# One-hots in three batches of 42, 42 and 41 slots a chunk with two buffers, in place of five of 25 with three; the gates' weights loaded later

## The reference

```python
h = relu(layernorm(x))                                    # layer 0
norm = clip(out_degree(src), 1, None) ** -0.5
x = x + relu(segment_sum((h * norm)[src], dst)) @ W.T + b
h = relu(layernorm(x))                                    # layer 1
msg = h[src] @ W_msg.T + b_msg + edge_embed[edge_type]    # 9 types
m = segment_sum(msg, dst)
r = sigmoid(m @ Wih_r.T + h @ Whh_r.T + biases)           # GRU cell
z = sigmoid(m @ Wih_z.T + h @ Whh_z.T + biases)
n = tanh(m @ Wih_n.T + b + r * (h @ Whh_n.T + b))
x = x + (1 - z) * n + z * h
```

## Time and profile before

| | |
|---|---|
| Runs | 997.35 us median of 3 (994.53 to 997.53) |
| Profiled execution | 993.72 us, its span 991.9 us |
| PE busy | 852.4 us, 86% |
| PEld busy | 758.8 us, 77% |
| DVE busy | 808.3 us, 81% |
| ACT busy | 515.5 us, 52% |
| POOL busy | 74.4 us, 8% |
| PE matmul groups | L1063 437.2 us, L1074 422.1, L1196 277.0 |
| Mean granted TensorE clock | 0.975 |

### The profile page before, as it was taken

The page is one execution under the profiler, slowest core; times in us unless marked ns, Lnnn a source line. Parts: engine busy times, 40 slices in busy tenths (PEclk is TensorE's granted clock), DMA queues, the critical chain, the costliest instruction groups (busy, mean ns, idle before and its releaser), DMA issues.

```text
span 991.9 us, 21125 instructions
## 1 busy us (share of the span) xinstructions
PE 852.4 (86%) x8908; PEld 758.8 (77%) x8908; DVE 808.3 (81%) x1177; ACT 515.5 (52%) x1051; POOL 74.4 (8%) x71
## 2 busy tenths in 40 slices
PE   1333599898998998989989999989999999999993
PEld 1222488787887887878878888969888889888882
DVE  5959999999999999999999995267766667766666
ACT  2896278687886886868868887211111111111110
POOL 5860100100101001000000000000000000000000
PEclk9999889999999999999999999999999999999997
DMA  4623315443434544333534330266667776666740
GB/s 108 143 68 130 132 50 221 159 159 136 159 141 159 227 174 159 137 137 147 212 134 187 140 141 7 60 237 242 245 245 266 280 269 245 241 246 260 280 162 12
DMA packets 38739, 169.99 MB, mean 171 GB/s; under 512 B 8156, under 2 KB 21667, under 8 KB 35696
## 3 DMA queue, kind: packets, MB, share of 16 engines
q1 hardware_dynamic: 32486, 161.48, 43.2%
q0 software_dynamic: 6000, 6.48, 2.8%
q10 hardware_dynamic: 154, 0.64, 0.2%
HBM read 88.52 MB, written 80.00 MB: 170 GB/s over the span
## 4 chain that ended last, share of the span: by engine, by line
PE 55%; DVE 29%; ACT 11%; issue 3%; DMA 2%; SPq 0%; DVEq 0%
PE ps L1196 25%; PE ps L1074 13%; DVE work L691 9%; DVE work L698 7%; PE ps L1063 7%; ACT ring L881 5%; DVE work L704 2%; PE ps L1162 2%; PE ps L1163 2%; ACT junk L893 2%; DMA tab<-dst 1%; PE ps L1086 1%; PE ps L1167 1%; PE ps L1166 1%; PE ps L1100 1%
## 5 line engine op out<-in xcount | busy, mean ns | idle before, releaser
L1063 PE MATMUL ps<-work 128*128 128x106 f16 x3125 | 437.2, 217 | 86.4 <-ACT ring L881 66.9
L1074 PE MATMUL ps<-ring,tab 125*128 125x250 f16 x2500 | 422.1, 275 | 1.9 <-DVE tab L676 1.2
L881 ACT ACTIVATE ring<-ps 128x848 f16<-128x848 f32 x375 | 330.0, 882 | 98.1 <-PE ps L1063 92.2
L1063 PEld LDWEIGHTS ps<-work 128*128 128x128 f16 x3125 | 291.4, 102 | 108.0 <-ACT ring L881 67.2
L1196 PE MATMUL ps<-ring,tab 125*128 125x250 f16 (+1 forms) x2500 | 277.0, 269 | 0.0
L1074 PEld LDWEIGHTS ps<-ring,tab 125*128 125x128 f16 x2500 | 246.9, 99 | 28.5 <-DVE tab L676 1.5
L1196 PEld LDWEIGHTS ps<-ring,tab 125*128 125x128 f16 (+1 forms) x2500 | 242.6, 97 | 28.8 <-issue 0.3
L691 DVE TENSOR_TENSOR work<-iota_lo,mch 128x3150 f16<-128x3150 f16 x125 | 224.4, 1795 | 26.0 <-PE ps L1063 13.6
L698 DVE TENSOR_TENSOR work<-iota_w,mch 128x1250 f16<-128x1250 f16 x250 | 193.9, 817 | 0.0
L778 DVE TENSOR_TENSOR work<-work,ring 125x3250 f16<-125x3250 f16 (+1 forms) x92 | 161.8, 1779 | 0.0
L1018 ACT ACTIVATE raw<-ps,bg 128x250 f32<-128x250 f32 x50 | 20.7, 466 | 174.9 <-PE ps L1163 174.9
(11 more groups left out here) (156 smaller groups left out, 608.9 us busy)
## 6 DMA issues: line engine op xcount, KB each, us to landing
adjacency<-ring SPq DMA_DIRECT2D x23, 2937.5 KB
ring<-adjacency SPq DMA_DIRECT2D x46, 812.5 KB, 6.3
ring<-adjacency SPq DMA_DIRECT2D x46, 750.0 KB, 8.8
adjacency<-ring SPq DMA_DIRECT2D x23, 183.1 KB
h_turned<-hst SPq DMA_DIRECT2D x25, 125.0 KB, 2.0
raw<-h_turned SPq DMA_DIRECT2D x25, 125.0 KB, 2.0
out<-x_sb SPq DMA_DIRECT2D x25, 125.0 KB
x_sb<-x SPq DMA_DIRECT2D x4, 560.0 KB
```

What stands on the lines that cost most here:

```text
L881: act.activation(to(x * 2 * u, 2, x), ps[:, s:s + 2, 0:x * SLOTS].rearrange("p b (x h) -> p h b x", h=SLOTS), ACT.Copy).then_inc(sem("evac ...
L1063: last = pe.matmul(ps[:, 2 * (u % 2) + i // BANKW, o:o + WCOLS], lohot[:, s, k, :], combo[:, s, k, :], start=True, stop=True)
L1074: mm = pe.matmul(psD[c % 2], tabv[0][P, h, s, :], adj[c % 2][P, h, :], start=i == 0, stop=i == 2 * BLOCKS - 1)
```

## The change

A batch of one-hots has 42, 42 and 41 slots instead of five times 25, and `work` holds two batches instead of three. What was hung on VectorE's five batches is laid on three: post0_x after batch 1, post0_norm after batch 2, the searches and splits of chunks 0 and 1 regrouped; the unpacking still takes one step after each batch, so that two steps come at the end of the chunk. TensorE's layer-0 products keep their old places (`QUOTA`). Chunk 1's fields are turned after window 84 and moved by ScalarE after unit 11. `wih_sb` and `whh_sb` lose their own tiles: they lie in `raw`, and SyncE loads them at the start of `sync_layer1`, before `dst`; the first gates wait for them (`gates_in`). The GRU's work tiles move from `raw` into `early`, and the small tiles of the search for heads (`head_q`, `head_row`, `head_node`, `totals`) into `early` too, with the same instructions on them.

```diff
@@ -27,12 +27,13 @@
 WCOLS = WIN * SLOTS
-BATCH = 25
-BATCHES = CHWIN // BATCH
+BATCH = 42
+BATCHES = (CHWIN + BATCH - 1) // BATCH
+QUOTA = 25
 BANKW = 4
...
 UNITS = (CHWIN + UNIT - 1) // UNIT
-HOTS = 3
+HOTS = 2
 AHEAD = 3
@@ -244,19 +239,28 @@
         bias_rest, at = carve(early, at, D)
...
         unsorted = early[:, at:at + PARTE // 2].bitcast(F16)
+        at += PARTE // 2
...
         h0 = tabs[1][:, :].bitcast(F32).rearrange("p (b f) -> p b f", f=D)
+        rz, at = carve(early, at, 2, CH)
+        msgs, at = carve(early, at, CH)
+        nin, at = carve(early, at, CH)
+        nn, at = carve(early, at, CH)
+        hnew, at = carve(early, at, CH)
+        h1c, at = carve(early, at, 2, CH)
...
         words = raw[:, :, :].rearrange("p g n -> p (g n)").bitcast(F32)
-        rz, at = carve(words, 0, 2, CH)
-        msgs, at = carve(words, at, CH)
-        nin, at = carve(words, at, CH)
-        nn, at = carve(words, at, CH)
-        hnew, at = carve(words, at, CH)
-        h1c, at = carve(words, at, 2, CH)
+        wih_sb, whh_sb = words[:, 0:3 * D], words[:, 3 * D:6 * D]
         counted_n = work[:, 0:BLOCKS * CH // 2].bitcast(F16)
@@ -364,8 +368,7 @@
                 load_x(sp, k)
-            for to, a in ((w0_sb, w0t), (wih_sb, wiht), (whh_sb, whht)):
-                sp.dma_start(to[:, :], a).then_inc(sem("later_in"), 16)
+            sp.dma_start(w0_sb[:, :], w0t).then_inc(sem("later_in"), 16)
             sp.wait_ge(sem("scaled"), 1)
@@ -402,6 +405,9 @@
         def sync_layer1(sp):
+            sp.wait_ge(sem("fields"), CHUNKS)
+            for to, a in ((wih_sb, wiht), (whh_sb, whht)):
+                sp.dma_start(to, a).then_inc(sem("gates_in"), 16)
             sp.wait_ge(sem("used0"), CHUNKS)
@@ -685,24 +691,25 @@
                 positive(v, sem("spent"), (BATCHES - 1) * before + k + 1)
-            at = slice(BATCH * b, BATCH * (b + 1))
+            n = min(BATCH, CHWIN - BATCH * b)
+            at = slice(BATCH * b, BATCH * b + n)
             lo2, col2 = (mch[:, par, k, at, :] for k in range(2))
...
             ch.did(v.tensor_tensor(
-                lohot[:, s, :, 0:even].rearrange("p k (n t) -> p k n t", t=2),
+                lohot[:, s, 0:n, 0:even].rearrange("p k (n t) -> p k n t", t=2),
                 iota_lo[:, 0:even].rearrange("p (n t) -> p n t", t=2).unsqueeze(1)
-                    .broadcast_to([128, BATCH, even // 2, 2]),
-                lo2.unsqueeze(2).broadcast_to([128, BATCH, even // 2, 2]), ALU.is_equal))
+                    .broadcast_to([128, n, even // 2, 2]),
+                lo2.unsqueeze(2).broadcast_to([128, n, even // 2, 2]), ALU.is_equal))
             for d in range(WIN):
...
                 ch.did(v.tensor_tensor(
-                    combo[:, s, :, cols].rearrange("p k (n t) -> p k n t", t=2),
+                    combo[:, s, 0:n, cols].rearrange("p k (a t) -> p k a t", t=2),
                     iota_w[:, cols].rearrange("p (n t) -> p n t", t=2).unsqueeze(1)
-                        .broadcast_to([128, BATCH, BLOCKS // 2, 2]),
-                    col2.unsqueeze(2).broadcast_to([128, BATCH, BLOCKS // 2, 2]), ALU.is_equal))
+                        .broadcast_to([128, n, BLOCKS // 2, 2]),
+                    col2.unsqueeze(2).broadcast_to([128, n, BLOCKS // 2, 2]), ALU.is_equal))
             ch.wait(but=WIN)
-            v.tensor_tensor(typehot[:, s, :, :, :],
-                            iota_t[:, :, :].unsqueeze(1).broadcast_to([128, BATCH, 1 + WIN, TB]),
+            v.tensor_tensor(typehot[:, s, 0:n, :, :],
+                            iota_t[:, :, :].unsqueeze(1).broadcast_to([128, n, 1 + WIN, TB]),
                             mch_s[:, par, :, at, :].rearrange("p m k t -> p k m t"),
@@ -734,13 +741,12 @@
                     if c == 0:
+                        if b == 0:
+                            search_runs(v, ch, 2)
                         if b == 1:
-                            search_runs(v, ch, 2)
+                            unpack(v, ch, 1, 2)
+                            search_runs(v, ch, 3)
                         if b == 2:
-                            unpack(v, ch, 1, 2)
-                        if b == 3:
-                            search_runs(v, ch, 3)
-                        if b == 4:
                             for m in range(4):
@@ -751,15 +757,17 @@
                             rows_vector(v, ch, 2)
-                        if b >= 1:
-                            split_rows(v, ch, b - 1)
-                        if b == 3:
+                        if b == 1:
+                            split_rows(v, ch, 0)
+                            split_rows(v, ch, 1)
                             rows_vector(v, ch, 3)
+                    if c >= 2 and b == 1:
+                        post0_x_vector(v, ch, c - 2)
                     if c >= 2 and b == 2:
-                        post0_x_vector(v, ch, c - 2)
-                    if c >= 2 and b == 4:
                         post0_norm_vector(v, ch, c - 2)
                 if c == 1:
+                    split_rows(v, ch, 2)
+                    split_rows(v, ch, 3)
                     rows_vector(v, ch, 4)
@@ -973,7 +981,7 @@
                     evacuate(act, c, u)
-                    if c == 0 and u == 13:
+                    if c == 0 and u == 11:
                         for _ in steps:
@@ -1080,7 +1088,7 @@
             if k == 0:
-                pe.wait_ge(sem("later_in"), 48)
+                pe.wait_ge(sem("later_in"), 16)
                 pe.wait_ge(sem("bias_parts"), 1)
@@ -1116,32 +1124,29 @@
                     build_window(pe, c, w)
-                    if c == 0 and w == 4 * BATCH - 1:
+                    if c == 0 and w == 2 * BATCH:
                         turn_tensor(pe, 1)
...
                         turn_tensor(pe, c + 1)
-                    if c == 1 and w % BATCH == BATCH - 1 and w >= 2 * BATCH - 1:
-                        t = w // BATCH - 1
-                        if t == 0:
+                    if c == 1 and w in (2 * BATCH - 1, CHWIN - 1):
+                        if w < CHWIN - 1:
                             pe.wait_ge(sem("evac"), UNITS)
-                        pe.wait_ge(sem("tab0"), 2 * t + 2)
-                        product0(pe, 0, 2 * TBATCH * t, 2 * TBATCH * (t + 1))
+                        for t in ((0, 1) if w < CHWIN - 1 else (2, 3, 4)):
+                            pe.wait_ge(sem("tab0"), 2 * t + 2)
+                            product0(pe, 0, 2 * TBATCH * t, 2 * TBATCH * (t + 1))
                     if c >= 2 and w >= 12:
...
                             positive(pe, sem("aggr"), c - 2)
-                        b, k = divmod(w, BATCH)
-                        to = (SENT[1] * (k - 11) // (BATCH - 12) if b == 0 else
-                              SENT[b] + (SENT[b + 1] - SENT[b]) * (k + 1) // BATCH)
+                        b, k = divmod(w, QUOTA)
+                        to = (SENT[1] * (k - 11) // (QUOTA - 12) if b == 0 else
+                              SENT[b] + (SENT[b + 1] - SENT[b]) * (k + 1) // QUOTA)
                         product0(pe, c - 1, sent, to)
...
                         POST0[w](pe, c - 2)
-                if c == 1:
-                    pe.wait_ge(sem("tab0"), 2 * (BLOCKS // TBATCH))
-                    product0(pe, 0, 2 * BLOCKS - 2 * TBATCH, 2 * BLOCKS)
             post0_low_tensor(pe, CHUNKS - 3)
@@ -1155,6 +1160,8 @@
             positive(pe, sem("nin"), m)
+            if m == 0:
+                pe.wait_ge(sem("gates_in"), 32)
             pe.wait_ge(sem(f"h1c_in{m % 2}"), 16 * (m // 2 + 1))
...
```

More of the change, by code:

```diff
@@ L57 @@
 heads_in weights_in emb_rows_in dst_in x_in0 x_in1 x_in2 x_in3 x_in4 ends_set ends_in
-iotas consts consts0 headhots hist totals counted rows_i bias_parts later_in cand_in0 cand_in1 cand_in2 cand_in3 cand_in4 cand_in5 run_i
+iotas consts consts0 headhots hist totals counted rows_i bias_parts later_in gates_in cand_in0 cand_in1 cand_in2 cand_in3 cand_in4 cand_in5 run_i
 runs_in0 runs_in1 runs_in2 runs_in3 runs_in4 runs_in5
@@ L176, in gnn @@
         heads_i = sb("heads_i", [LO, HPART], I32)
[L177 to L180, removed]
         cnt = sb("cnt", [128, CHUNKS], F32)
@@ L203, in gnn @@
         bm_sb = sb("bm_sb", [128, D], F32)
-        wih_sb = sb("wih_sb", [128, 3 * D], F32)
-        whh_sb = sb("whh_sb", [128, 3 * D], F32)
         bg_i = sb("bg_i", [128, 3], F32)
@@ L246, in gnn @@
         bias_rest, at = carve(early, at, D)
+        head_q, at = carve(early, at, HPART)
+        head_q = head_q[P, :]
+        head_row, at = carve(early, at, HPART)
+        head_row = head_row.bitcast(F16)[P, :].rearrange("p (j t) -> p j t", t=2)
+        head_node, at = carve(early, at, HPART)
+        head_node = head_node.bitcast(F16)[P, :].rearrange("p (j t) -> p j t", t=2)
+        totals, at = carve(early, at, CHUNKS)
         raw_dst, at = carve(early.bitcast(I32), 0, PARTE + 1)
         unsorted = early[:, at:at + PARTE // 2].bitcast(F16)
+        at += PARTE // 2
```

(15 more changed lines are left out.)

## The result

The changed kernel takes 998.3 us (median of 17 runs, 996.7 to 1000.3), the kernel before 996.0 beside it (17 runs, 994.4 to 997.5): ratio 1.0021, 95% interval 1.0014 to 1.0028. It is slower by 2.3 us, where I had forecast 2 us faster.

The account below looks back on a forecast made before the run. TensorE and VectorE were nearly full, TensorE bounding plain chunks. Terms -3.4 (chunks 3 to 24), +1.5 (clock), -2.2 (opening), +2.0 (weights) made -2.1, called -2, from 997.35 to 995.4 us; 8-in-10 range 985 to 1002.

Parts of the forecast that it names:

- The chain of waits: In plain chunks: buffer release, batch 2, norm, h1s, then window 88, the last two 0.75 us late.
- the clock's term: TensorE's granted clock falling after pauses of about 2 us in six heavy chunks: +1.5 us, bounds 0 and +7.2.
- what chunks 3 to 24 save: Plain chunks, heavy chunks and chunk 22 together, before the clock: -3.4 us.
- Plain chunks: Chunks 3 to 24 without the heavy ones and 22: later norm makes 20.76 us of 20.01, 15 times, +11.2 us.
- Heavy chunks: Six chunks (4, 7, ... 19) where VectorE also unpacks edges for three: 22.36 us before clock against 24.87, -15.0 us.
- Chunk 22: The chunk that unpacks for one chunk only: 21.3 us against 20.9, +0.4 us.
- rival 3: Windows 88 to 100 of heavy chunks: clock falls in all six, 1.2 us each, 1001 us; chance 0.18.
- The weights: Gates' weights loaded after the build ahead of dst, delaying TensorE's first gates: +2 us, bounds +0.5 and +6.
- The opening: Chunks 0 to 2: earlier turn of chunk 1's fields against longer first batches, -2.2 us, bounds -5 and +2.
- Rival 1: Later norm costs nothing in plain chunks, so the 11.2 us go: 984 us; chance 0.15.
- Rival 2: Heavy chunks keep their pause near 3.5 us through VectorE's backlog, the -15.0 shrinks to near nothing: 1007 us; chance 0.07.
- Rival 4: Weights land late, TensorE waits 5 us at the first gates: +2.5 on the forecast, 998 us; chance 0.10.

Follow-up runs that it names:

- the filled pause: Changed kernel with eight spare matmuls of 500 columns before window 88 of chunks 4, 7, ... 19: 993.6 us, ratio to before 0.9982.
- the shift: h1s and the steps behind it one unit later on ScalarE and TensorE, in both kernels: changed kernel 983.8 us, kernel before 990.7 us.
- early weights: Changed kernel with the gates' weights loaded in the last chunk of the build instead of ahead of dst: 995.8 us, ratio to before 1.0001.
- the later turn: Changed kernel with chunk 1's fields moved by ScalarE after unit 13 again, not 11: 1004.3 us, ratio to before 1.0087.
- the last kernel above: Changed kernel with h1s one unit later, weights loaded in the build's last chunk, and norm ahead of the third unpacking step: 992.4 us.

## Why the prediction was wrong

The chain of waits was right and so were the places. The sign was lost in the sizes of a small sum: the step that failed is the clock's term, put at +1.5 us where it measures 4.7. With that term right and the others as forecast the sum is +1.1. Next comes what chunks 3 to 24 save, -3.4 forecast and -0.8 measured: plain chunks took 1.7 of it and heavy ones 0.8. Term by term:

- **Plain chunks** (+0.75 forecast, +0.86 measured, so 12.9 us in place of 11.2). The chain release, batch 2, norm, h1s, window 88 is there link by link. The mis-sized link is L711: 0.49 us to the next instruction (202.39 to 202.88), where I scaled L704's 0.24 to 0.39. L698 and L705 came to 5.08 against my 5.06.
- **Heavy chunks** (22.36 forecast, 22.49 measured at full clock). The pause was to be "about 2 us" and is 1.84. Chunk 22 was to take 21.3 and took 21.28. Chunks 3 to 24 take 469.1 us in the kernel with the filled pause, in which the clock doesn't fall, 0.8 less than before's 469.9 with its six falls, where I had 3.4 less.
- **The clock, the step that failed most.** I took +1.5 of bounds 0 and 7.2, "on the side of the shorter pause". The filled pause gives 4.7. The argument was that shorter waits had left the clock alone; but those were 1.2 us and less, and in the busy chunks of the trace no pause stood between 1.2 and 3.5 us. The middle of the bounds, 3.6, would have been the honest value, and rival 3 was nearer to the truth than I gave it.
- **The weights** (+2 forecast, +2.5 and +2.9 measured). SyncE's two issues took 0.97 us (639.97 to 640.94) for the 0.8 forecast; the bytes in front of dst and h_turned cost the other 1.5 to 1.9, where I allowed 1.2.
- **The opening** (-2.2 forecast, -2.7 by the two profiles of each). Turning the fields two units earlier was sized at 5.4 and measures 6.0 in medians, 4.4 in the profiles of this stretch (120.3 against 115.9).

With these the sum is -0.8 + 4.7 + 2.7 - 2.7 = +3.9, against +2.3 measured. The 1.6 between them is of the size by which one profile differs from another (the opening of before differs by 1.3 between its two), and is left open.

**The rivals.** Rival 1, that the later norm costs nothing in plain chunks, is refuted by the wait of 0.75 in every one of them, and by the shift. Rival 2, heavy chunks that keep their pause of 3.5, is refuted by 1.84 (its own terms add up to 1009, not 1007). Rival 3, the clock falling in each, is half true: three or four of six, 4.7 of its 7.2 us. Rival 4 is written so that its wait (5 us for 3.24 + 2) doesn't give its own +2.5; the wait that would is 7.7 us. Measured are 6.65, a part of the way from the forecast's 5.2. The Trainium skill's sentence on the gate ("TensorE: Matmul & The Clock Gate", "What's actually happening"), that its watch does not start with the kernel, fits the trace without being proved by it: equal pauses of 1.84 and 1.85 us had different outcomes.

**Where the gain went.** With room for the norm the changed kernel is 6.9 us faster than the kernel before with the same room (983.8 and 990.7), though it still carries the late weights. In the profiles of the two, chunks 3 to 24 take 459.3 and 466.4 us, and five falls of the clock at 1.4 us are 7.0 of these 7.2. At full clock a cycle of three chunks takes the same, 63.00 and 63.07, though VectorE is busy for 61.0 of it instead of 62.1. So the saving on VectorE did not shorten the cycle. It split TensorE's one pause of 2.17 us: in the changed kernel it waits 0.50 us for L711 at window 84 of the heavy chunk, 0.80 at window 96 and 1.03, in place of 0.28, at the next chunk's first window. The three short pauses left the clock up where the long one mostly did not. Without the room the saving in heavy chunks was paid out again in plain ones, because a coarser release let the last batch start later, and norm stands behind it.

## What to carry to other kernels

When batches grow and buffers shrink, list what stands behind the last batch on that engine and who waits for it: the release of the buffer now sets the time of that work too, even where the batches themselves arrive in time. A wait that several engines share (pnm, h1s, window 88) without slack in the common case is the first thing to give room; it cost one unit's shift and was worth 14.5 us here. Compare two kernels at the same granted clock before you put a gain down to less work: here nearly all of a lead of 7.2 us in chunks 3 to 24 was the clock. Where a forecast is a small difference of large terms, a term with bounds of 0 and 7 belongs in the middle unless a row lies near one end.

## What the runs showed of the hardware

- The granted clock can turn an idle pause into a longer one: a pause of 1.84 us cost 1.2 to 1.4 us more in the chunks where the clock fell to 0.50 after it (22.49 against 23.7 to 23.9). Filling it with eight useless matmuls (1.85 us in their row) gained 4.7 us over the run.
- The outcome depended on more than the pause's length. Pauses of 1.84 us brought the clock down in four of six heavy chunks in after, and in every second one in its second profile and in those with early weights and with the later turn; pauses of 2.17 us in five of six in the kernel before with the shift; one of 2.25 us a cycle in six of six in the last kernel above, and 3.48 in six of six in before, both with cycles of 64.9 us. After pauses of 0.8 to 1.26 us a cycle it never fell. No run here separates the length of the pause from its place in time.
- Two DMAs of 192 KB each, put ahead of one of 806 KB on SyncE's queue, made TensorE wait 2.6 to 3.2 us longer for the transfer behind them (6.65 against 4.09, 6.46 against 3.24) and cost 2.5 to 2.9 us in medians.
